# Projection stage of a two-layer image kernel: the low part of every odd unit computed by VectorE from PSUM, of every even unit by TensorE and ScalarE

## The reference

```
xn = layernorm(x)                                  # over the 64 channels
left  = (xn @ left_w  + left_b)  * mask * sigmoid(xn @ lgate_w + lgate_b)
right = (xn @ right_w + right_b) * mask * sigmoid(xn @ rgate_w + rgate_b)
out_gate = sigmoid(xn @ ogate_w + ogate_b)
out = einsum('bkjd,bkid->bijd', left, right)       # a 512x512x512 product for each of 64 channels
x = x + (layernorm(out) @ out_w + out_b) * out_gate
```

## Time and profile before

| what | us |
|---|---|
| median of 3 runs | 3029.33 (3028.93 to 3033.02) |
| the profiled execution's own time | 3029.29 |
| its span | 3027.5 |
| `project`: first matmul of the stage to the last value | about 240 to 1092 |
| PE busy over the span | 2510.4 (83%) |
| VectorE busy | 2207.5 (73%) |
| ScalarE busy | 1372.8 (45%) |
| GpSimd busy | 1020.9 (34%) |

### The profile page before, as it was taken

How to read it: one execution, slowest core, us unless ns; L and a number is a source line. 1 busy time by engine, 2 the same in 40 slices (tenths; PEclk the granted TensorE clock), 3 DMA queues, 4 the chain that set the end, 5 groups by cost and what they waited for, 6 DMA issues and landing times. The chain is left out here.

```text
span 3027.5 us, 40932 instructions
## 1 busy us (share of the span) xinstructions
PE 2510.4 (83%) x12694; PEld 1864.6 (62%) x12694; DVE 2207.5 (73%) x3463; ACT 1372.8 (45%) x1778; POOL 1020.9 (34%) x1042
## 2 busy tenths in 40 slices
PE   0008999889889979999999992989988988789775
PEld 0005666556556658888888881556655655588664
DVE  5998888778778748888888885766766766226453
ACT  0006888778778857666766671212211221100000
POOL 1018888778778800000000000444444444300000
PEclk9999999999999989999999996999999999769988
DMA  9845999788779767777777773999999999749999
GB/s 375 341 188 192 341 337 336 287 307 314 284 294 336 285 256 280 275 282 285 281 277 280 284 263 129 389 379 379 377 372 371 380 386 364 247 163 393 418 419 406
DMA packets 260650, 950.26 MB, mean 314 GB/s; under 512 B 31153, under 2 KB 31665, under 8 KB 260146
## 3 DMA queue, kind: packets, MB, share of 16 engines
q1 hardware_dynamic: 226160, 877.25, 76.7%
q10 hardware_dynamic: 34370, 71.54, 6.1%
HBM read 540.83 MB, written 407.90 MB: 313 GB/s over the span
## 5 line engine op out<-in xcount | busy, mean ns | idle before, releaser
L1104 POOL TENSOR_TENSOR fi_square_sum<-fi_square_sum,fi_square 128x1024 f32<-128x1024 f32 x128 | 302.7, 2365 | 429.0 <-ACT fi_square L1075 429.0
L780 PE MATMUL ct_acc_ps<-ct_l_hi,ct_r_hi 128*128 128x512 f32 x1024 | 404.3, 395 | 20.6 <-ACT ct_l_hi L794 20.6
L652 DVE SCALAR_TENSOR_TENSOR pj_lr<-pj_v_ps,layer_b_val,pj_sig 128x1024 f32<-128x1024 f32 x256 | 328.8, 1284 | 121.7 <-ACT pj_sig L589 118.4
L1075 ACT ACTIVATE fi_square<-fi_x 128x1024 f32<-128x1024 f32 x128 | 135.4, 1057 | 600.5 <-DVE fi_x L1132 590.9
L781 PE MATMUL ct_acc_ps<-ct_l_lo,ct_r_hi 128*128 128x512 f32 x1024 | 404.2, 395 | 0.0
L782 PE MATMUL ct_acc_ps<-ct_l_hi,ct_r_lo 128*128 128x512 f32 x1024 | 404.1, 395 | 0.0
L1031 PE MATMUL fi_y_ps<-fi_scaled,layer_w_bd 128*128 128x512 f32 x512 | 282.1, 634 | 71.1 <-DVE fi_scaled L1115 70.9
L490 POOL TENSOR_TENSOR front_ring<-front_ring,layer_gn_shift 128x512 f32<-128x512 f32 x256 | 333.5, 1304 | 5.5 <-DVE front_ring L618 5.5
L1115 DVE TENSOR_TENSOR fi_scaled<-fi_m,fi_s_ps 128x512 f32<-128x512 f32 x256 | 174.0, 680 | 190.5 <-DMA fi_m<-mixed_d 162.5
L589 ACT ACTIVATE pj_sig<-pj_g_ps,layer_b_gate 128x1024 f32<-128x1024 f32 x256 | 285.5, 1115 | 43.0 <-PE pj_g_ps L555 40.5
L1302 PE MATMUL la_ps_ps<-la_col,la_inv_cols 128*128 128x256 f32 x1024 | 243.3, 400 | 46.5 <-DVE la_early L1372 28.0
(11 more groups left out here) (183 smaller groups left out, 5035.8 us busy)
## 6 DMA issues: line engine op xcount, KB each, us to landing
lr_d<-pj_lr SPq DMA_DIRECT2D x128, 1024.0 KB, 5.8
gate_d<-pj_gout SPq DMA_DIRECT2D x128, 512.0 KB, 6.8
ct_l<-lr_d SPq DMA_DIRECT2D x64, 1024.0 KB, 7.1
ct_r<-lr_d SPq DMA_DIRECT2D x64, 1024.0 KB, 9.0
mixed_d<-ct_o SPq DMA_DIRECT2D x64, 1024.0 KB, 4.9
fi_m<-mixed_d SPq DMA_DIRECT2D x128, 512.0 KB, 14.1
fi_g<-gate_d SPq DMA_DIRECT2D x128, 512.0 KB, 12.9
fi_x<-in_x SPq DMA_DIRECT2D x32, 2048.0 KB, 9.1
```

Of the source, the lines that this page charges most:

```text
L652: dve.scalar_tensor_tensor(out=out[:, :, RG * (m % 2):RG * (m % 2) + RG], in0=v_ps[:, :].rearrange("p (q i) -> p q i", i=RG), scalar=keep. ...
L780: pe.matmul(bank, high, l_hi[b][:, :, k, :], start=(k == 0), stop=False)
L1104: pool.tensor_tensor(square_sum[:, :, :], square_sum[:, :, :], square[:, :, :], ALU.add).then_inc(sum_done, 1)
```

## The change

Odd units (m % 2 == 1) get their low part from one VectorE instruction that reads the PSUM buffer and the high part and writes `low[1]`. PE's subtraction and ScalarE's copy are left for even units. The semaphore `low_ready` becomes two, one for each parity, and the counts are taken by pairs. VectorE's new instruction for unit n+1 stands in slot n (even), after the statistics and the first guess and ahead of the value of n.

```diff
-        low_ready = t.sem("low_ready")
+        low_even = t.sem("low_even")
+        low_odd = t.sem("low_odd")
...
+        def pairs_before(n, m, j, ahead):
+
+            if is_int(n):
+                return (n + ahead) // 2
+            return (UB * RING // 2) * j + (m + ahead) // 2
...
-            def transposes(n, m):
+            def transposes(n, m, j):
                 pe.wait_ge(xn_ready, n + 1)
-                at_least(pe, low_ready, n - 1)
+                at_least(pe, low_odd if m % 2 else low_even, pairs_before(n, m, j, 0))
...
                 if inside(n + 2):
-                    transposes(n + 2, m + 2)
-                if inside(n + 1):
-                    subtract_high(n + 1, m + 1)
+                    transposes(n + 2, m + 2, j)
+                if inside(n + 1) and m % 2 == 1:
+                    subtract_high(n + 1, m + 1, j)
                 if inside(n):
-                    pe.wait_ge(low_ready, n + 1)
+                    pe.wait_ge(low_odd if m % 2 else low_even, pairs_before(n, m, j, 0) + 1)
...
-            def copy_rest(n, m):
-                act.wait_ge(rest_ready, n + 1)
+            def copy_rest(n, m, j):
+                act.wait_ge(rest_ready, pairs_before(n, m, j, 0) + 1)
                 at_least(act, vals_in, n - 1)
-                act.activation(low[m % 2][:, :], x_ps[m % 2][:, :], ACT.Copy).then_inc(low_ready, 1)
+                act.activation(low[0][:, :], x_ps[0][:, :], ACT.Copy).then_inc(low_even, 1)
...
-                if inside(n + 1):
-                    copy_rest(n + 1, m + 1)
+                if inside(n + 1) and m % 2 == 1:
+                    copy_rest(n + 1, m + 1, j)
...
+            def subtract_high(n, m):
+                dve.wait_ge(high_ready, n + 1)
+                at_least(dve, vals_in, n - 1)
+                dve.tensor_tensor(low[1][:, :], x_ps[1][:, :], high[m % 4][:, :], ALU.subtract).then_inc(low_odd, 1)
+
...
+                if inside(n + 1) and m % 2 == 0:
+                    subtract_high(n + 1, m + 1)
                 if inside(n):
                     value(n, m, j)
```

More of the change, by code:

```diff
@@ L534, in transposes, with subtract_high @@
                 last.then_inc(turned, 1)
-            def subtract_high(n, m):
+            def subtract_high(n, m, j):
                 pe.wait_ge(high_ready, n + 1)
```

## The result

The changed kernel takes 3134.11 us in the median (3125.55 to 3141.57), the kernel before 3029.13 in the same runs: ratio **1.0356**, 95% interval 1.0335 to 1.0378, +105 us. The forecast was 3151 in a range of 3120 to 3200. The profiled execution took 3125.55 us with a span of 3123.8; it is the shortest of the four. The stage itself grew by 106.8 us in the two profiles (841.6 to 948.4, from the first value to the last).

What follows compares the result with a forecast made beforehand. PE was taken to bound the kernel before. With the round of waits binding, 119 pairs lose 1.045 us each (+124.4) and some 8 gain 0.32 (-2.6): together +122 on 3029.3 gives 3151, range 3120 to 3200.

Steps and rivals of the forecast that it cites:

- PE sets the pace before: Steady projection: PE is busy 100% of the time and its starts add up to the 3.11 us a unit takes.
- By sums alone VectorE's load would fit: VectorE's own work per pair of units, with the new subtraction, is 6.16 us, below the present 6.22.
- The round closes at 7.12 us a pair: Waits from PE's transposes through sigmoid, VectorE's queue and new subtraction back to PE's transposes sum to 7.12, against 6.22.
- The first guess adds 0.58 every fourth pair: In every fourth pair VectorE's first guess stands ahead of the subtraction, adding 0.58 us; the average round becomes 7.27.
- PE stands still 1.22 us a pair, 1.80 with the first guess: PE idles ahead of every odd slot's transposes: 7.12 - 5.90 = 1.22 us, or 1.80 with the first guess.
- PE's saving of 0.32: PE loses one subtraction per pair of units, 0.32 us, so its own work falls from 6.22 to 5.90 us.
- The four stops stay and cost the same: VectorE's idle times at the returns of the loop over 32 units stay; their added cost was taken as 0.
- Rival 1, the clock: PE's clock falls in the new pauses: at 32 longer ones +49 us, chance 0.11; at all 128 +197, chance 0.02.
- Rival 2, faster: VectorE's or PE's own sum binds, not the round: a pair costs 6.16, -10 us, 3019; chance 0.07.
- Rivals 3 and 4: Only the output gate's product waits: +35 us, 3064, chance 0.05; PE was not the bound: stays 3029, chance 0.02.

Runs made afterwards that it cites:

- experiment 7: Kernel before, without any subtraction for odd units (their products read a tile of zeros instead), plus 31 memsets at the start: 2957.16 us, ratio 0.9781.
- experiment 3: Kernel before plus a VectorE operation of the subtraction's size at its place, its result read by nothing: 2994.74 us, ratio 0.9915.
- experiments 5 and 6: Experiment 5, and the changed kernel with its subtraction at the slot's head plus 225 or 97 memsets at program start: 2977.30 and 2972.25 us.
- experiment 5: Changed kernel plus 225 tiny VectorE memsets at the very start of the program: 3109.57 us, ratio 1.0285.

## Why the prediction was right, and where not

- *PE sets the pace before.* Right: experiment 7 takes work from PE alone and the time falls by 27 us.
- *By sums alone VectorE's load would fit.* Nearly. It was added up as 6.16 us against 6.22; the unused operation costs 14 us, 0.11 a pair. Work that fits in the sum still arrives late in single slots. The first guess and an operation fall in the same slot, and PE's value product then waits for VectorE's value: 8 times from 350 to 540 us in experiment 3, once in eight units, 0.2 to 0.3 us each, where PE had no such wait before.
- *The round closes at 7.12 us a pair.* Measured 7.07. Two legs were off and made up for each other: the statistics to the next instruction took 0.80 and not 0.92 (the first guess, from which the 0.92 was read, waits for the statistics' result, the subtraction does not), and from VectorE's end to PE's start it was 0.14 and not 0.05.
- *The first guess adds 0.58 every fourth pair.* It adds 0.73: eight units take 29.01 us (transposes at 367.60 and 396.61 us), less three rounds of 7.07 is 7.80. The average is 7.25 a pair; 7.265 was forecast. That these two agree so closely is luck in part: the round was put 0.05 too long and the first guess 0.15 too short.
- *PE stands still 1.22 us a pair, 1.80 with the first guess.* Measured 1.04 and 1.72 to 1.94.
- *PE's saving of 0.32.* The term was mis-sized: 0.23. It hardly counts in the forecast, because the round bound, not PE, but it would have been 0.09 too much in any forecast of a gain.
- *The four stops stay and cost the same.* Wrong, and this is the step that made 3151 too high. They were taken as VectorE's own idle time, with a cost that could only grow with the loop. Their cost hangs on where the loop's code lies: in the stage of before they cost 45.7 us (841.6 - 795.9). The changed stage is 948.4 us long (249.5 to 1197.9); less the 795.9 without stops, the round's 122.6 and some 2 for two falls of the clock outside the stops, 28 are left, 18 less than before. So the 106.8 by which the stage grew are 122.6 for the round, 2 for the clock and -18 for the stops. The direct comparison says the same: without stops the changed stage is 22.9 us shorter (925.5), though it has three more of the clock's falls in it.
- *Rival 1, the clock.* It had 0.13 as a case of its own and came partly: five falls without stops and two outside the stops in the changed kernel, not 32, and some 1.0 to 1.8 us each, where 1.54 was reckoned. The pauses that were followed by one were all of the long kind.
- *Rival 2, faster.* The change doesn't do it, but with the subtraction at the head of the slot it is what happens: 6 to 10 us, where 10 was summed. The mechanism was right and the order excluded it.
- *Rivals 3 and 4.* PE's idle time lies ahead of the transposes and not ahead of the output gate's product, so the wait was not a partial one; and experiment 7 shows that PE was the bound.
- The Trainium skill's rule in "VectorE: DVE Perf Modes", section "Rules for kernel authors", to minimise the count of chained operations and not the semaphores, doesn't price this case, where the wait goes across engines: the count is the same in experiments 5 and 6, and the place of one operation between its waits makes 132 us (3109.57 against 2977.30, both with 225 memsets).

## What to carry to other kernels

When work is moved to another engine, put it where its input is ready and its reader waits, not where the code reads well: follow the round reader, reader's readers, back to the moved instruction, and add up what stands ahead of it in its queue. Sums of busy time said "fits" here for three places of which one costs 4%. And before two versions of a kernel with a hardware loop are compared, look for idle time put down to issue right after the loop's returns, and for instruction packets in the DMA queues at those times: a few dozen instructions more or less ahead of the loop can be worth more than the change under test.

## What the runs showed of the hardware that was not expected

- The hardware loop on VectorE stopped at each of its four returns, without any wait of the program: 4.6 to 5.7 us, and in some places of the code another 3.6 to 3.8. 32 tiny instructions ahead took away all four stops, 38 us of 3022; 128 took away nothing. In the kernels with stops the queue of instruction packets was at work in the loop (15 packets of 8 KB from the first return to the last), in those without it was not.
- PE's granted clock fell behind five of 26 pauses of 1.7 to 2.1 us (experiment 5), and behind none of the 78 pauses of about 1 us between them.
- A VectorE result reached a waiting group of transposes 0.14 us after its end, a waiting value product 0.05 us.
